# A routed feed-forward kernel: the high and low part of w2 side by side, streamed by one matmul of 512 columns

## The chip, the cores and the metric

The kernel runs on one core of one Trainium2 chip. A core has a matrix engine (TensorE: PE for its matmuls and PEld for its weight loads in the profile), VectorE (DVE), ScalarE (ACT), GpSimd (POOL), SyncE (SP), and 16 DMA engines. The metric is the device time of one execution in microseconds (us), as the median of several runs; lower is better. Durations of single instructions come from one profiled execution.

## The reference

A modulated linear layer makes a hidden vector for each of 8192 tokens; a router picks 2 of 8 experts for each token; each expert keeps at most 2560 tokens, runs a two-layer network on them, and the weighted result is added to the input.

```python
ys = cond * scale; d = rsqrt((ys * ys) @ (weight * weight) + EPS)
hidden = (x * ys[:, None, :]) @ weight * d[:, None, :]        # T = 8192 rows, D = 256
logits = hidden @ wr.T                                         # E = 8 experts
vals, idx = top_k(logits, 2);  gating = softmax over the two
dispatch = first cap (2560) tokens of each expert, in order of token
h = gelu(xg @ w1[e] + b1[e])                                   # F = 1024
y = h @ w2[e] + b2[e]                                          # D = 256
out = x + segment_sum(y * gate, dispatch)
```

## The kernel before

**Two stages.** Up to about 180 us of the profile the kernel makes the hidden rows, routes them, and writes a table of slots. After that it works through blocks of 256 slots (SLOTS, that is SUBS = 2 halves of 128 rows), expert by expert. Here there are 69 blocks, 8 or 9 of them for each of the 8 experts. The change lies in this second stage.

**Precision.** Weights and activations are split in two float32r parts: hi is the rounded value and lo the rest. A product takes three matmuls that add into the same PSUM columns: hi by hi, hi by lo and lo by hi (lines 522 to 524 for the first layer, 538 to 540 for the second).

**One block on TensorE** (`one_block`, line 547). Four transposes (line 512) bring in the rows of the next block. `first_product(f)`, for f = 0 to 7, makes 128 columns of h in a PSUM bank: 6 matmuls of 256 columns. `second_product(f)` adds the contribution of chunk f to y: for each of the two halves s the three matmuls 538 to 540, each with h as the loaded operand (128 rows) and 256 columns of w2 streamed, into `y_bank[s]` (banks 2 and 3, columns 0 to 255). A block has 48 + 48 such matmuls. The last matmul of f = 7 signals `y_done` for its half. The last two products of a block stand after the first two `first_product` of the next block. `second_product(0)` waits for `h_ready` of chunks 0 and 1 of its block (line 555); it is also what overwrites `y_bank`.

**The other engines.** ScalarE applies gelu to each bank of h twice (line 641, raw and hi). VectorE makes h_lo (line 902), then signals `h_ready`. At the end of a block VectorE's order, written by hand, is: h_lo of chunk 0 of the next block; for each half s wait for `y_free` and `y_done`, then y = bank + b2 (line 926); h_lo of chunk 1 of the next block (on which TensorE's `second_product(0)` waits); y times the gate (line 932), which signals `y_ready`.

**The way out** is GpSimd's (`one_block`, line 382, for each block): copy the slot numbers (line 370), issue the scatter-add of half 0 into the output (line 356), list the block three ahead (lines 331 and 332), issue its two gathers (line 323), issue the scatter-add of half 1 (line 356), wait until both adds have landed, and only then signal `y_free` (line 364). `y_sb` is single: VectorE's line 926 of a block waits for the landing of the block before.

**Weights.** In the first two blocks of an expert ScalarE (line 603) and VectorE (line 716) split the weights of the next expert from `w_raw`, 512 columns at a time, in 8 pieces. After the last piece SyncE loads the weights of the expert after that, 2 MB, into `w_raw`.

Of the kernel before, what the change touches and what calls it, by code (L numbers as in the profile page):

```python
# [24 lines left out]
P = 128  # L25
# [4 lines left out]
KC = D // P  # L30
# [20 lines left out]
PIECE = 512  # L51
PIECES = 2 * WCOLS // PIECE
PAD = SUBS * P
NO_SLOT = float(1 << 22)
# [3 lines left out]
def build(nc, x, cond, w, wr_t, w1, b1_t, w2, b2, ident, tri, expert_low, slot_base, token_ids,  # L58
# [12 lines left out]
    with ExitStack() as ctx:  # L71
# [69 lines left out]
        w_raw = sb("w_raw", [P, 2 * WCOLS])  # L141
        w_hi = [sb(f"w_hi{u}", [P, 2 * WCOLS], F32R) for u in range(2)]
        w_lo = [sb(f"w_lo{u}", [P, 2 * WCOLS], F32R) for u in range(2)]
        table_sb = sb("table", [P, COLS, 2], I32)
# [12 lines left out]
        h_hi = [sb(f"h_hi{i}", [P, SLOTS], F32R) for i in range(RING)]  # L157
        h_lo = [sb(f"h_lo{i}", [P, SLOTS], F32R) for i in range(RING)]
        y_sb = [sb(f"y{s}", [P, D]) for s in range(SUBS)]

# [53 lines left out]
        h_ready = sem("h_ready")  # L214
        y_done = sem("y_done")
        y_biased = sem("y_biased")
        y_ready = sem("y_ready")
# [9 lines left out]

        FILLING = GROUPS - 3

        def plan_of(eng, e):  # L230
# [198 lines left out]
        def _(pe):  # L429
# [86 lines left out]
            def first_product(u, f):  # L516

                h = h_bank[f % RING][:, 0:SLOTS]
                for k in range(KC):
                    cols = slice(k * F + f * P, k * F + (f + 1) * P)  # L520
                    rows = slice(k * SLOTS, (k + 1) * SLOTS)
                    pe.matmul(h, w_hi[u][:, cols], xt_hi[:, rows], start=(k == 0), stop=False)  # L522
                    pe.matmul(h, w_hi[u][:, cols], xt_lo[:, rows], start=False, stop=False)  # L523
                    mm = pe.matmul(h, w_lo[u][:, cols], xt_hi[:, rows], start=False, stop=(k == KC - 1))  # L524
                if f == FC - 1:
                    mm.then_inc(xt_used, 1)
                if f < RING:

                    mm.then_inc(h_open, 1)

            def second_product(u, f):

                cols = slice(WCOLS + f * D, WCOLS + (f + 1) * D)
                for s in range(SUBS):
                    hi = h_hi[f % RING][:, s * P:(s + 1) * P]
                    lo = h_lo[f % RING][:, s * P:(s + 1) * P]
                    y = y_bank[s][:, 0:D]
                    pe.matmul(y, hi, w_hi[u][:, cols], start=(f == 0), stop=False)  # L538
                    pe.matmul(y, hi, w_lo[u][:, cols], start=False, stop=False)  # L539
                    mm = pe.matmul(y, lo, w_hi[u][:, cols], start=False, stop=(f == FC - 1))  # L540
                    if f == FC - 1:
# [49 lines left out]
        def _(act):  # L591
# [7 lines left out]
            def split_piece(u, i, n_loaded):  # L599
                if i == 0:  # L600
                    act.wait_ge(w_loaded, n_loaded)
                cols = slice(i * PIECE, (i + 1) * PIECE)
                act.copy(w_hi[u][:, cols], w_raw[:, cols]).then_inc(w_hi_done, 1)

# [67 lines left out]
        def _(dve):  # L672
# [40 lines left out]
            def split_piece(u, i, count):  # L713
                cols = slice(i * PIECE, (i + 1) * PIECE)
                dve.wait_ge(w_hi_done, count)
                dve.tensor_tensor(w_lo[u][:, cols], w_raw[:, cols], w_hi[u][:, cols].bitcast(F32),
                                  ALU.subtract).then_inc(w_lo_done, 1)

# [193 lines left out]
            def one_block(u, e, b, tile, piece0):  # L912
# [9 lines left out]

                for s in range(SUBS):
                    dve.wait_ge(y_free, b * SUBS + (s + 1))
                    dve.wait_ge(y_done, b * SUBS + (s + 1))
                    dve.tensor_tensor(y_sb[s][:, :], y_bank[s][:, 0:D], b2_sb[:, bass.ds(e * D, D)],  # L926
                                      ALU.add).then_inc(y_biased, 1)
                split_chunk(b + 1, 1)
# [61 lines left out]
```

## Time and profile before

| what | us |
|---|---|
| median of 3 runs | 1146.6 |
| lowest and highest run | 1142.14, 1147.25 |
| span of the profiled execution, first to last instruction | 1087.6 |
| busy in that span: TensorE matmul, weight load | 986.6 (91%), 931.1 (86%) |
| busy: VectorE, ScalarE, GpSimd | 520.4 (48%), 552.6 (51%), 548.7 (50%) |

The median lies 59.0 us above the profiled span; that is time around the first and the last instruction that no row shows. A matmul's recorded duration (0.28 us here) includes its way through the array, and the next one starts before it ends: what a matmul costs in a stream is the distance from its start to the next one's. So a busy share of TensorE near 100% says that something was in the array, not that it was streaming at its peak. In brackets behind a row of the timeline stands the idle time of the engine before the row, and what ended it.

### The profile page before, as it was taken

What the parts mean: (1) busy time and instruction counts of PE and PEld (TensorE: products, weight loads), DVE (VectorE), ACT (ScalarE), POOL (GpSimd) and SP (SyncE); (2) the same over time, 40 slices, a digit from 0 to 9 for tenths busy, and PEclk for the clock granted to TensorE, in tenths of its full rate; (3) what the DMA queues carried; (4) which work ended last, traced back from release to release, by engine and by line L of the source; (5) the groups of instructions that cost most, each with busy time, mean ns of one, the idle gap of its engine ahead of it and who ended that gap; (6) DMA issues with size and microseconds to landing.
All of it is one profiled execution on the core that took longest, in us unless ns stands there. A gap on an engine that the chain in (4) does not pass through costs nothing.

```text
span 1087.6 us, 24164 instructions
## 1 busy us (share of the span) xinstructions
PE 986.6 (91%) x7652; PEld 931.1 (86%) x7653; DVE 520.4 (48%) x1555; ACT 552.6 (51%) x1312; POOL 548.7 (50%) x617
## 2 busy tenths in 40 slices
PE   6988883889989999899989998999899989999995
PEld 4656653789989999899989998999899989999995
DVE  5766664434454445344544444445444544345442
ACT  3111012646655657455646665556466655556553
POOL 0677777644444455344445454444445544445553
PEclk9888885989999999899989999999899999999998
DMA  8745415232242223322242224222422242222222
GB/s 281 242 146 174 136 60 166 75 72 43 39 117 39 43 48 80 69 44 43 39 116 39 44 47 111 43 43 39 116 39 43 43 115 44 43 39 39 40 47 29
DMA packets 70686, 83.62 MB, mean 77 GB/s; under 512 B 10944, under 2 KB 63680, under 8 KB 70528
## 3 DMA queue, kind: packets, MB, share of 16 engines
q0 software_dynamic: 30784, 36.86, 20.7%
q1 hardware_dynamic: 30064, 37.58, 10.5%
q10 hardware_dynamic: 9824, 9.03, 2.4%
q8 instruction: 5, 0.08, 0.0%
q14 instruction: 9, 0.07, 0.0%
HBM read 47.65 MB, written 35.69 MB: 77 GB/s over the span
## 4 chain that ended last, share of the span: by engine, by line
issue 31%; DMA 26%; POOL 22%; PE 7%; DVE 5%; POOLq 5%; DVEq 2%; SPq 1%; ACT 0%
DMA out_rows<-sb_y,sb_add_ids 24%; POOL sb_xg L323 8%; POOL table L316 6%; POOL sb_gather_ids L331 5%; DVE sb_y L932 2%; DVEq L932 2%; POOLq L331 2%; POOL sb_ids_ring L332 1%; PE bank L538 1%; POOL sb_add_ids L370 1%; PE bank L539 1%; PE bank L540 1%; DVE sb_y L926 1%; DMA table<-sb_pay,sb_slots 1%; DMA out_rows<-sb_x 1%
## 5 line engine op out<-in xcount | busy, mean ns | idle before, releaser
L641 ACT ACTIVATE sb_h_raw<-bank,sb_b_now 128x256 f32<-128x256 f32 x554 | 263.4, 475 | 370.0 <-PE bank L540 192.4
L902 DVE TENSOR_TENSOR sb_h_lo<-sb_h_raw,sb_h_hi 128x256 fp32r<-128x256 f32 x554 | 230.6, 424 | 301.5 <-ACT sb_h_hi L641 290.1
L538 PE MATMUL bank<-sb_w_hi,sb_h_hi 128*128 128x256 f32 x1104 | 318.5, 289 | 22.5 <-DVE sb_h_lo L902 22.2
L522 PE MATMUL bank<-sb_xt_hi,sb_w_hi 128*128 128x256 f32 x1108 | 322.7, 291 | 8.1 <-DVE sb_h_lo L902 5.4
L524 PE MATMUL bank<-sb_xt_hi,sb_w_lo 128*128 128x256 f32 x1108 | 315.3, 285 | 0.0
L523 PE MATMUL bank<-sb_xt_lo,sb_w_hi 128*128 128x256 f32 x1108 | 315.2, 284 | 0.0
L539 PE MATMUL bank<-sb_w_lo,sb_h_hi 128*128 128x256 f32 x1104 | 311.6, 282 | 0.0
L540 PE MATMUL bank<-sb_w_hi,sb_h_lo 128*128 128x256 f32 x1104 | 311.3, 282 | 0.0
L356 POOL DMA_INDIRECT out_rows<-sb_y,sb_add_ids x138 | 228.0, 1652 | 79.2 <-POOL sb_add_ids L370 53.0
L641 ACT ACTIVATE sb_h_hi<-bank,sb_b_now 128x256 fp32r<-128x256 f32 x554 | 259.7, 469 | 0.0
L538 PEld LDWEIGHTS bank<-sb_w_hi,sb_h_hi 128*128 128x128 f32 x1104 | 211.9, 192 | 32.3 <-DVE sb_h_lo L902 32.1
L522 PEld LDWEIGHTS bank<-sb_xt_hi,sb_w_hi 128*128 128x128 f32 x1108 | 213.3, 193 | 10.2 <-DVE sb_h_lo L902 7.0
L523 PEld LDWEIGHTS bank<-sb_xt_lo,sb_w_hi 128*128 128x128 f32 x1108 | 213.6, 193 | 0.0
L524 PEld LDWEIGHTS bank<-sb_xt_hi,sb_w_lo 128*128 128x128 f32 x1108 | 213.3, 192 | 0.0
L539 PEld LDWEIGHTS bank<-sb_w_lo,sb_h_hi 128*128 128x128 f32 x1104 | 211.4, 192 | 0.0
L540 PEld LDWEIGHTS bank<-sb_w_hi,sb_h_lo 128*128 128x128 f32 x1104 | 211.2, 191 | 0.0
L323 POOL DMA_INDIRECT sb_xg<-hidden,sb_gather_ids x134 | 135.3, 1010 | 83.2 <-POOL sb_ids_ring L332 55.7
L370 POOL COPY sb_add_ids<-sb_ids_ring 128x2 int32 x69 | 16.5, 239 | 299.6 <-DVE sb_y L932 299.6
L316 POOL DMA_INDIRECT table<-sb_pay,sb_slots x128 | 125.3, 979 | 68.1 <-issue 37.5
L926 DVE TENSOR_TENSOR sb_y<-bank,sb_b 128x256 f32<-128x256 f32 x138 | 52.2, 420 | 176.2 <-POOLq L364 165.6
L471 PE MATMUL bank<-sb_xs_t,sb_w 128*128 128x512 f32 x128 | 66.2, 666 | 0.0
L613 ACT COPY sb_hid<-bank 128x512 f32<-128x512 f32 x32 | 17.2, 588 | 91.2 <-PE bank L491 91.2
(110 smaller groups left out, 778.4 us busy)
## 6 DMA issues: line engine op xcount, KB each, us to landing
sb_w_raw<-in_w SPq DMA_DIRECT2D x18, 1024.0 KB
out_rows<-sb_x SPq DMA_DIRECT2D x16, 512.0 KB
hidden<-sb_hid ACTq DMA_DIRECT2D x16, 512.0 KB
sb_x<-in_x SPq DMA_DIRECT2D x15, 512.0 KB
out_rows<-sb_y,sb_add_ids POOLq DMA_INDIRECT x138
sb_xg<-hidden,sb_gather_ids POOLq DMA_INDIRECT x134
table<-sb_pay,sb_slots POOLq DMA_INDIRECT x128
sb_b<-in_b SPq DMA_DIRECT2D x1, 1024.0 KB, 8.9
```

Source lines behind the costliest of these rows:

```text
L316: pool.indirect_dma_start(table, bass.IndirectOffsetOnAxis(slots[u][:, c, j:j + 1], axis=0), pay[u][:, c, j, :], None, bounds_check=TABLE ...
L323: pool.indirect_dma_start(into[:, s, :], None, hidden, bass.IndirectOffsetOnAxis(block_ids[:, s:s + 1], axis=0),).then_inc(landed, 16)
L331: pool.tensor_copy(gather_ids[:, :], ids)
L356: pool.indirect_dma_start(out, bass.IndirectOffsetOnAxis(add_ids[:, s:s + 1], axis=0), y_sb[s][:, :], None, compute_op=ALU.add,).then_inc( ...
L522: pe.matmul(h, w_hi[u][:, cols], xt_hi[:, rows], start=(k == 0), stop=False)
L523: pe.matmul(h, w_hi[u][:, cols], xt_lo[:, rows], start=False, stop=False)
L524: mm = pe.matmul(h, w_lo[u][:, cols], xt_hi[:, rows], start=False, stop=(k == KC - 1))
L538: pe.matmul(y, hi, w_hi[u][:, cols], start=(f == 0), stop=False)
L539: pe.matmul(y, hi, w_lo[u][:, cols], start=False, stop=False)
L540: mm = pe.matmul(y, lo, w_hi[u][:, cols], start=False, stop=(f == FC - 1))
L641: ins = act.activation(h[f % RING][:, :], h_bank[f % RING][:, 0:SLOTS], ACT.Gelu_apprx_tanh, bias=b1_now[u][:, f:f + 1])
L902: dve.tensor_tensor(h_lo[f % RING][:, :], h_raw[f % RING][:, :], h_hi[f % RING][:, :].bitcast(F32), ALU.subtract).then_inc(h_ready, 1)
```

## The change

w1 keeps its two buffers of hi and lo parts, now under names of their own. For w2 the hi and the lo part of each chunk f lie side by side in one buffer `w2_both[P, FC, 2, D]`, so that 512 columns follow one another. `second_product` streams those 512 columns through the loaded h_hi into the whole bank: columns 0 to 255 get hi by hi, columns 256 to 511 get hi by lo. A second matmul loads h_lo and adds lo by hi into the upper half. The output y is then the sum of the two halves of the bank and b2. VectorE first adds b2 to the upper half into a new tile `y_low` (waiting for `y_done` alone), for both halves s, and then adds `y_low` to the lower half into `y_sb` (waiting for `y_free`). Blocks stay at 256 slots; loops, gelu, the first product and GpSimd's program are as they were.

```diff
-        w_hi = [sb(f"w_hi{u}", [P, 2 * WCOLS], F32R) for u in range(2)]
-        w_lo = [sb(f"w_lo{u}", [P, 2 * WCOLS], F32R) for u in range(2)]
+        w1_hi = [sb(f"w1_hi{u}", [P, WCOLS], F32R) for u in range(2)]
+        w1_lo = [sb(f"w1_lo{u}", [P, WCOLS], F32R) for u in range(2)]
+        w2_both = [sb(f"w2_both{u}", [P, FC, 2, D], F32R) for u in range(2)]
...
+        def piece_of(u, i):
+
+            if i < W1_PIECES:
+                cols = slice(i * PIECE, (i + 1) * PIECE)
+                return w1_hi[u][:, cols], w1_lo[u][:, cols], w_raw[:, cols]
+            chunks = PIECE // D
+            f = (i - W1_PIECES) * chunks
+            raw = w_raw[:, i * PIECE:(i + 1) * PIECE].rearrange("p (c d) -> p c d", d=D)
+            return w2_both[u][:, f:f + chunks, 0, :], w2_both[u][:, f:f + chunks, 1, :], raw
...
             def second_product(u, f):
 
-                cols = slice(WCOLS + f * D, WCOLS + (f + 1) * D)
+                both = w2_both[u][:, f, :, :].rearrange("p v d -> p (v d)")
                 for s in range(SUBS):
                     hi = h_hi[f % RING][:, s * P:(s + 1) * P]
                     lo = h_lo[f % RING][:, s * P:(s + 1) * P]
-                    y = y_bank[s][:, 0:D]
-                    pe.matmul(y, hi, w_hi[u][:, cols], start=(f == 0), stop=False)
-                    pe.matmul(y, hi, w_lo[u][:, cols], start=False, stop=False)
-                    mm = pe.matmul(y, lo, w_hi[u][:, cols], start=False, stop=(f == FC - 1))
+                    pe.matmul(y_bank[s][:, :], hi, both, start=(f == 0), stop=False)
+                    mm = pe.matmul(y_bank[s][:, D:2 * D], lo, w2_both[u][:, f, 0, :], start=False, stop=(f == FC - 1))
...
                 for s in range(SUBS):
+                    dve.wait_ge(y_done, b * SUBS + (s + 1))
+                    dve.tensor_tensor(y_low[s][:, :], y_bank[s][:, D:2 * D], b2_sb[:, bass.ds(e * D, D)],
+                                      ALU.add).then_inc(y_begun, 1)
+                for s in range(SUBS):
+                    dve.wait_ge(y_begun, b * SUBS + (s + 1))
                     dve.wait_ge(y_free, b * SUBS + (s + 1))
-                    dve.wait_ge(y_done, b * SUBS + (s + 1))
-                    dve.tensor_tensor(y_sb[s][:, :], y_bank[s][:, 0:D], b2_sb[:, bass.ds(e * D, D)],
-                                      ALU.add).then_inc(y_biased, 1)
+                    dve.tensor_tensor(y_sb[s][:, :], y_bank[s][:, 0:D], y_low[s][:, :], ALU.add).then_inc(y_biased, 1)
```

On TensorE, `second_product(6)` at the end of a block, the kernel before:

```order
L538 MATMUL bank2<-sb_w_hi1,sb_h_hi2 128x256 [waits h_ready]
L539 MATMUL bank2<-sb_w_lo1,sb_h_hi2 128x256
L540 MATMUL bank2<-sb_w_hi1,sb_h_lo2 128x256
L538 MATMUL bank3<-sb_w_hi1,sb_h_hi2 128x256
L539 MATMUL bank3<-sb_w_lo1,sb_h_hi2 128x256
L540 MATMUL bank3<-sb_w_hi1,sb_h_lo2 128x256
```

and the changed one, with the first two matmuls of the next product behind it (its lines are numbered anew):

```order
L551 MATMUL bank2<-sb_w2_both1,sb_h_hi2 128x512 [waits h_ready]
L552 MATMUL bank2<-sb_w2_both1,sb_h_lo2 128x256
L551 MATMUL bank3<-sb_w2_both1,sb_h_hi2 128x512
L552 MATMUL bank3<-sb_w2_both1,sb_h_lo2 128x256
L536 MATMUL bank5<-sb_xt_hi,sb_w1_hi1 128x256
L537 MATMUL bank5<-sb_xt_lo,sb_w1_hi1 128x256
```

Six matmuls with six weight loads became four with four; the streamed columns are the same 1536.

On VectorE, at the end of a block, the kernel before:

```order
L902 TENSOR_TENSOR sb_h_lo0<-sb_h_raw0,sb_h_hi0 128x256 [waits gelu_done]
L924 ISA
L926 ISA [waits y_done,y_free]
L926 TENSOR_TENSOR sb_y0<-bank2,sb_b2 128x256
L924 REGISTER_ALU
L926 TENSOR_TENSOR sb_y1<-bank3,sb_b2 128x256 [waits y_done,y_free]
L901 REGISTER_ALU
L902 TENSOR_TENSOR sb_h_lo1<-sb_h_raw1,sb_h_hi1 128x256 [waits gelu_done]
```

and the changed one:

```order
L913 TENSOR_TENSOR sb_h_lo0<-sb_h_raw0,sb_h_hi0 128x256 [waits gelu_done]
L935 ISA
L936 ISA [waits y_done]
L936 TENSOR_TENSOR sb_y_low0<-bank2,sb_b2 128x256
L935 REGISTER_ALU
L936 TENSOR_TENSOR sb_y_low1<-bank3,sb_b2 128x256 [waits y_done]
L941 TENSOR_TENSOR sb_y0<-bank2,sb_y_low0 128x256 [waits y_free,y_begun]
L941 TENSOR_TENSOR sb_y1<-bank3,sb_y_low1 128x256 [waits y_free,y_begun]
L912 REGISTER_ALU
L913 TENSOR_TENSOR sb_h_lo1<-sb_h_raw1,sb_h_hi1 128x256 [waits gelu_done]
```

Two additions of the same size were put ahead of the two that were there; the wait for `y_free` now stands between them, and h_lo of chunk 1 stands behind all four.

## Rows read from the trace of the kernel before

**Rows 1.** Page, busy time of each engine with its share of the span, and instructions.

```profile
PE 986.6 (91%) x7652; PEld 931.1 (86%) x7653; DVE 520.4 (48%) x1555; ACT 552.6 (51%) x1312; POOL 548.7 (50%) x617
```

**Rows 2.** Waits of VectorE, 205 to 1088 us: total, times, longest.

```profile
DVE sb_y L926 <- POOLq L364: 165.6, 62, 6.4
...
DVE sb_y L926 <- POOLq L410: 7.4, 1, 7.4
DVE sb_y L926 <- PE bank L540: 3.2, 6, 0.5
```

**Rows 3.** Timeline of VectorE, 836 to 849 us: start, us, instruction, idle before.

```profile
836.35 0.76 DVE L926 TENSOR_TENSOR sb_y<-bank,sb_b 128x256 f32<-128x256 f32 x2 [2.49 <-POOLq L364]
...
837.39 0.82 DVE L932 TENSOR_SCALAR sb_y<-sb_y,sb_table 128x256 f32<-128x256 f32 x2
...
840.77 0.42 DVE L902 TENSOR_TENSOR sb_h_lo<-sb_h_raw,sb_h_hi 128x256 fp32r<-128x256 f32 x1 [0.99 <-ACT sb_h_hi L641]
...
848.59 0.42 DVE L926 TENSOR_TENSOR sb_y<-bank,sb_b 128x256 f32<-128x256 f32 x1 [2.46 <-POOLq L364]
```

**Rows 4.** Timeline of GpSimd, the same stretch.

```profile
838.05 0.20 POOL L370 COPY sb_add_ids<-sb_ids_ring 128x2 int32 x1 [4.00 <-DVE sb_y L932]
839.09 1.60 POOL L356 DMA_INDIRECT out_rows<-sb_y,sb_add_ids  x1 [0.84 <-POOL sb_add_ids L370]
...
840.23 0.99 POOL L332 COPY sb_ids_ring<-sb_table  x1
842.11 1.01 POOL L323 DMA_INDIRECT sb_xg<-hidden,sb_gather_ids  x1 [0.88 <-POOL sb_ids_ring L332]
...
844.70 1.61 POOL L356 DMA_INDIRECT out_rows<-sb_y,sb_add_ids  x1 [0.30 <-issue]
```

**Rows 5.** Timeline of TensorE, 834 to 838 us.

```profile
834.35 0.28 PE L540 MATMUL bank<-sb_w_hi,sb_h_lo 128*128 128x256 f32 x1
...
835.77 0.28 PE L524 MATMUL bank<-sb_xt_hi,sb_w_lo 128*128 128x256 f32 x1
...
837.49 0.38 PE L538 MATMUL bank<-sb_w_hi,sb_h_hi 128*128 128x256 f32 x1 [0.30 <-DVE sb_h_lo L902]
```

**Rows 6.** Line 471 (float32, 512 columns): TensorE, 90 to 94 us.

```profile
90.56 3.60 PE L471 MATMUL bank<-sb_xs_t,sb_w 128*128 128x512 f32 x8
```

**Rows 7.** Timeline of VectorE's line 926, from one expert's first blocks to the next one's.

```profile
324.47 0.76 DVE L926 TENSOR_TENSOR sb_y<-bank,sb_b 128x256 f32<-128x256 f32 x2 [6.09 <-POOLq L364]
...
337.05 0.78 DVE L926 TENSOR_TENSOR sb_y<-bank,sb_b 128x256 f32<-128x256 f32 x2 [0.53 <-PE bank L540]
...
349.43 0.76 DVE L926 TENSOR_TENSOR sb_y<-bank,sb_b 128x256 f32<-128x256 f32 x2 [1.20 <-POOLq L364]
...
361.54 0.76 DVE L926 TENSOR_TENSOR sb_y<-bank,sb_b 128x256 f32<-128x256 f32 x2 [1.60 <-POOLq L364]
...
373.65 0.75 DVE L926 TENSOR_TENSOR sb_y<-bank,sb_b 128x256 f32<-128x256 f32 x2 [2.00 <-POOLq L364]
...
386.02 0.76 DVE L926 TENSOR_TENSOR sb_y<-bank,sb_b 128x256 f32<-128x256 f32 x2 [2.58 <-POOLq L364]
```

**Rows 8.** Windows: engines' busy time (instructions), TensorE's granted clock, DMA share, GB/s.

```profile
320.00:324.00 4.00, 1.86 (x15) 1.59 (x14) 0.00 (x0) 1.48 (x4) 0.00 (x0) 0.97 0.89 278
324.00:328.00 4.00, 2.63 (x13) 2.39 (x12) 2.28 (x7) 0.70 (x2) 1.03 (x2) 0.50 0.01 2
```

**Rows 9.** Timeline of TensorE, 328 to 330 us, at the lower granted clock.

```profile
328.34 0.41 PE L538 MATMUL bank<-sb_w_hi,sb_h_hi 128*128 128x256 f32 x1
328.56 0.41 PE L539 MATMUL bank<-sb_w_lo,sb_h_hi 128*128 128x256 f32 x1
```

**Rows 10.** Timeline of GpSimd, 361 to 374 us: the copy of line 332.

```profile
365.45 0.75 POOL L332 COPY sb_ids_ring<-sb_table  x1
```

**Rows 11.** Timeline of VectorE, the last block.

```profile
1074.90 0.77 DVE L926 TENSOR_TENSOR sb_y<-bank,sb_b 128x256 f32<-128x256 f32 x2 [0.53 <-PE bank L540]
```

More of the change, by code:

```diff
@@ L52 @@
 PIECES = 2 * WCOLS // PIECE
+W1_PIECES = WCOLS // PIECE
 PAD = SUBS * P
@@ L158, in build @@
         h_lo = [sb(f"h_lo{i}", [P, SLOTS], F32R) for i in range(RING)]
+        y_low = [sb(f"y_low{s}", [P, D]) for s in range(SUBS)]
         y_sb = [sb(f"y{s}", [P, D]) for s in range(SUBS)]
@@ L215, in build @@
         y_done = sem("y_done")
+        y_begun = sem("y_begun")
         y_biased = sem("y_biased")
@@ L521, in first_product @@
                     rows = slice(k * SLOTS, (k + 1) * SLOTS)
-                    pe.matmul(h, w_hi[u][:, cols], xt_hi[:, rows], start=(k == 0), stop=False)
-                    pe.matmul(h, w_hi[u][:, cols], xt_lo[:, rows], start=False, stop=False)
-                    mm = pe.matmul(h, w_lo[u][:, cols], xt_hi[:, rows], start=False, stop=(k == KC - 1))
+                    pe.matmul(h, w1_hi[u][:, cols], xt_hi[:, rows], start=(k == 0), stop=False)
+                    pe.matmul(h, w1_hi[u][:, cols], xt_lo[:, rows], start=False, stop=False)
+                    mm = pe.matmul(h, w1_lo[u][:, cols], xt_hi[:, rows], start=False, stop=(k == KC - 1))
                 if f == FC - 1:
@@ L601, in split_piece @@
                     act.wait_ge(w_loaded, n_loaded)
-                cols = slice(i * PIECE, (i + 1) * PIECE)
-                act.copy(w_hi[u][:, cols], w_raw[:, cols]).then_inc(w_hi_done, 1)
+                hi, _, raw = piece_of(u, i)
+                act.copy(hi, raw).then_inc(w_hi_done, 1)
             for i in range(PIECES):
@@ L713, in split_piece @@
             def split_piece(u, i, count):
-                cols = slice(i * PIECE, (i + 1) * PIECE)
+                hi, lo, raw = piece_of(u, i)
                 dve.wait_ge(w_hi_done, count)
-                dve.tensor_tensor(w_lo[u][:, cols], w_raw[:, cols], w_hi[u][:, cols].bitcast(F32),
-                                  ALU.subtract).then_inc(w_lo_done, 1)
+                dve.tensor_tensor(lo, raw, hi.bitcast(F32), ALU.subtract).then_inc(w_lo_done, 1)
             dve.wait_ge(const_in, 16 * CONSTS)
```

## The prediction

> **What bounds the kernel now.** The page comes first, and it misleads. TensorE is busy 91% of the span and its weight loads 86%, every other engine about half [rows 1]. Read alone, that says TensorE is the bound and every nanosecond taken off its stream is time won. So the second view is the waits, and there VectorE's line 926, the step that takes a finished block out of the bank. It needs two things: `y_done` (TensorE has finished the block) and `y_free` (the scatter-adds of the block before have landed). In 62 of 69 blocks the later of the two was GpSimd's signal, 165.6 us of waiting in all; one more is the first block, released once by line 410. Only in 6 blocks was TensorE the later one, and all 6 together waited 3.2 us, at most 0.5 us each [rows 2]. 62 + 1 + 6 is all of them. The reader should see that TensorE, busy as it looks, is early nearly always.
>
> The third view is one turn of what is late instead. From line 926 at 836.35 us to the next at 848.59 us is 12.24 us [rows 3]. In between: the gate at 837.39 [rows 3], GpSimd's copy at 838.05, the add of half 0 issued at 839.09, the first gather at 842.11, the add of half 1 at 844.70 [rows 4], and 3.9 us later both adds have landed and the next 926 starts. Nothing in this circle is a matmul. TensorE's own work for a block is 96 matmuls at a distance of 0.118 us (834.35 to 835.77 us is twelve starts [rows 5]), 11.3 us, and with the four transposes 11.7 us. That is 0.5 us less than the turn; TensorE takes the difference as a wait for h_lo of chunk 1, which stands behind 926 (the row at 837.49 [rows 5]). In that turn the last matmul of `second_product(7)` started at 834.35 and ends its 0.28 us at 834.63; 926 started 1.7 us later.
>
> TensorE leads only in short episodes. After an expert's first two blocks SyncE loads 2 MB of weights; in 320 to 324 us the DMA share is 0.89 at 278 GB/s, and after it TensorE's granted clock is 0.50, the 1.2 GHz level [rows 8]. The adds land late, 926 waits 6.09 us, TensorE stands, and the next block starts at the low clock, so that its 926, at 337.05, is released by TensorE after 0.53 us of idling. From then on TensorE, at 11.7 us a block, runs ahead of the circle again: the idle time before 926 is 1.20, 1.60, 2.00, 2.58 us [rows 7].
>
> **The change part by part.** *Removed on TensorE:* 2 weight loads and 2 matmuls in each `second_product`, while the streamed columns stay the same. A group of three costs 3 x 0.118 = 0.353 us now. At the lower clock the distance is 0.22 us, as read to two places (328.34 to 328.56 [rows 9]), about 256 cycles of 1.2 GHz (0.213 us): one column a cycle. At the upper clock 256 columns need 0.107 us, so 0.011 us of each 0.118 is not streaming. The trace has no float32r matmul of 512 columns. The lower bound is pure streaming, 0.213 us; the upper is twice the narrow one, 0.236 us; a middle, 0.219 us, takes 0.353 to 0.337 us and saves 0.016 us a group (bounds 0 and 0.023). A farther bound is line 471, whose float32 matmuls of 512 columns leave two records each in the trace, 8 records in 3.60 us, 0.45 us a record [rows 6]; with it a group would cost 0.57 us. I exclude most of that because those need more than one pass, and the float32r ones of rows 9 need one. So TensorE's work falls by 16 x 0.016 = 0.26 us a block, 69 x 0.26 = 18 us in all. Where the circle leads, this turns into idle time before 926 and is worth nothing. The cover is 1.7 us of lead in the steady turn.
>
> *Added on VectorE:* two additions a block, ahead of the wait for `y_free`. Two of this shape take 0.76 us together, the second starting 0.34 us after the first [rows 3]. Behind them stand the final additions, h_lo of chunk 1 (TensorE waits for it), the gate, and behind that GpSimd. Where the idle time before 926 is 1.2 us or more, they fit into it: 0.53 us until half 0 is done, 0.36 us (three matmuls) until half 1 is, 0.34 us to the next start is 1.23 us. That holds for 63 of 69 blocks, and costs nothing there beyond a few hundredths. In the 6 TensorE-led blocks the final addition starts 0.36 + 0.34 = 0.70 us later than it did, less the 0.02 us that the old pair lost waiting for half 1 (0.78 instead of 0.76 us [rows 7]), less what TensorE gained since it was last released: about 0.15 us in the five after a weight load, where part of the block runs at the low clock (a group is 768 cycles either way), and 0.26 us in the last block of all, which is led by TensorE too [rows 11]. Net 5 x (0.68 - 0.15) + (0.68 - 0.26) = 3.1 us **later**.
>
> *Moved:* GpSimd's copy at line 332 takes 0.99 us in the steady turn [rows 4], where VectorE's line 902 at 840.77 us [rows 3] falls into it, and 0.75 us in a turn where TensorE is less far ahead [rows 10]. The turns show it: 361.54 to 373.65 is 12.11 us, 373.65 to 386.02 is 12.37 us; the step comes when the idle time before 926 passes about 2 us [rows 7]. After the change TensorE reaches that lead sooner (0.26 us more a block, and 0.5 us more because the led block ended later), so one short turn fewer after each of the five episodes: 5 x 0.25 = 1.2 us later. The new additions read one operand from PSUM; the rule for this is in the Trainium skill, SBUF — State Buffer, section Who interferes with whom: a VectorE instruction with two SBUF inputs contends with a GpSimd one that reads SBUF, one with a single SBUF input does not. Rows 4 and 10 agree on line 902, which has two; no row shows the new pair beside a copy. By the rule it costs GpSimd nothing.
>
> *The split of w2* writes the same 512 columns in two pieces of 256 and stays as long. SyncE's and GpSimd's programs are untouched. Buffers are as large as before.
>
> Sum: + 3.1 + 1.2 = + 4.3 us on the profiled span of 1087.6 us, 1091.9 us. The median of the runs stands 59.0 us above that span, and the change touches none of that: 1146.6 + 4.3 = **1150.9 us**.
>
> **The rivals.** *TensorE is the bound after all.* Then all 18 us come out at the end: 1146.6 - 18 = 1129 us. For it speaks rows 1; against it rows 2, where a TensorE that were infinitely fast could remove 3.2 us of waiting before 926. The Trainium skill (Perfetto Trace Analysis, section Identifying the Most-Contended Engine) says to optimize first the engine with the highest occupancy and to judge TensorE by its weight-load share; by that rule this rival would be the forecast, and the waits of this trace disagree. Chance 0.09.
>
> *The low clock lasts longer (the other side).* In the window at 324 us TensorE is busy 2.63 of 4 us and at 0.50 [rows 8]. A shorter stream makes the idle time around each weight load longer by some 0.3 us. If one more stretch of about 3.5 us ran at 1.2 GHz after each of the 7 episodes, the block would lose half of it, 1.7 us. It decides there because TensorE leads, with 0.5 us and less to spare; in a steady turn the lead of 1.7 us would cover it. Price 7 x 1.7 = 12 us: 1163 us. Chance 0.08.
>
> *VectorE is late in every block.* If in the steady turn the new pair ended after `y_free`, the circle would grow by up to 0.7 us, 63 x 0.7 = 44 us: 1195 us. It needs `y_done` to come 1 us later than it does. Chance 0.02.
>
> *The wide matmul doesn't stream at one column a cycle.* At 0.45 us a group costs 0.57 us, TensorE's block 11.7 + 16 x 0.21 = 15.1 us, above 12.24: about 2.9 us x 69 = 200 us, 1347 us. The point from which it decides is a group of 0.353 + 0.53 / 16 = 0.386 us. Chance 0.02.
>
> **How the numbers follow.** A measurement of this kernel can tell about 0.5% from no change, 5.7 us: 1140.9 to 1152.3 us. The forecast case has 0.79. Its own bounds: with no saving in the wide matmul, + 1.0 us; with two short turns lost instead of one, + 1.2; with none of the new delay because the episodes fall differently in a run, - 4.3; the two runs farthest apart differ by 5.1 us, and a change in where line 902 meets the copies by 0.1 us a turn is 7 us either way. It therefore gives 1142 to 1159 us, and splits into 0.54 same, 0.23 slower, 0.02 faster. Adding the rivals: faster 0.11, same 0.54, slower 0.35. The range 1142 to 1160 leaves out the first rival, most of the second, and the two far ones.
>
> **What would show each step.** In the changed profile: TensorE's distance from line 551 to 552 near 0.219 us and from 552 on near 0.118; TensorE's and the weight loads' busy shares lower; the idle time before the final additions still ended by line 364 in some 62 blocks; turns of 12.1 to 12.4 us, as before; the first additions started before `y_free` in those; the final additions 0.5 us later in the blocks after a weight load. I am wrong if turns are shorter than 12.1 us in number, which would mean that TensorE's work reaches the circle by a way I have not seen, or if they are longer than 12.4 us outside the episodes.

## The result and the profile after

| | kernel before | changed kernel |
|---|---|---|
| median of 16 runs each, us | 1143.6 | 1148.8 |
| profiled execution, us (its span) | not known (1087.6) | 1150.9 (1149.1) |

The ratio of the two, runs on the same chips against each other, is **1.0053, 95% interval 1.0031 to 1.0076**: about 6 us slower (the two medians are 5.2 us apart). One of the 16 runs of the changed kernel took 1898.6 us and is not in the ratio. The forecast was 4.3 us slower, 1150.9 us. It started from the three runs of before shown then, whose median was 1146.6 us; with 13 more it is 1143.6.

The page of the changed kernel, to be read against [rows 1]:

```profile
PE 1002.7 (87%) x6548; PEld 892.0 (78%) x6549; DVE 574.0 (50%) x1693; ACT 553.8 (48%) x1312; POOL 549.7 (48%) x617
```

1104 matmuls and weight loads fewer, and VectorE has 138 instructions and 53.6 us more. The busy shares tell nothing of the time: TensorE's work fell and the kernel got slower. VectorE's waits, the counterpart of [rows 2] (us in total, times, longest), 260 to 1149 us:

```profile
DVE sb_y L941 <- POOLq L378: 103.9, 61, 5.5
...
DVE sb_y_low L936 <- PE bank L552: 29.6, 66, 0.6
```

The final addition (line 941) is still released by GpSimd's signal (line 378) in 61 blocks. What was one wait of 165.6 us is now a short wait for TensorE ahead of the new additions (line 936) and a shorter one for GpSimd behind them. One turn, VectorE, 324 to 328 us (start, us, instruction, idle before), beside [rows 3]:

```profile
324.41 0.78 DVE L936 TENSOR_TENSOR sb_y_low<-bank,sb_b 128x256 f32<-128x256 f32 x2 [0.45 <-PE bank L552]
...
326.49 0.76 DVE L941 TENSOR_TENSOR sb_y<-bank,sb_y_low 128x256 f32<-128x256 f32 x2 [1.30 <-POOLq L378]
327.16 0.41 DVE L913 TENSOR_TENSOR sb_h_lo<-sb_h_raw,sb_h_hi 128x256 fp32r<-128x256 f32 x1
327.54 0.82 DVE L946 TENSOR_SCALAR sb_y<-sb_y,sb_table 128x256 f32<-128x256 f32 x2
```

The new pair has ended 1.30 us before the final additions start, so it is hidden there, as forecast. TensorE, 650 to 652 us, beside [rows 5]:

```profile
650.78 0.50 PE L551 MATMUL bank<-sb_w_both,sb_h_hi 128*128 128x512 f32 x1 [0.43 <-DVE sb_h_lo L913]
...
651.23 0.39 PE L551 MATMUL bank<-sb_w_both,sb_h_hi 128*128 128x512 f32 x1
651.46 0.28 PE L552 MATMUL bank<-sb_w_both,sb_h_lo 128*128 128x256 f32 x1
651.58 0.28 PE L536 MATMUL bank<-sb_xt_hi,sb_w_hi 128*128 128x256 f32 x1
```

The second wide matmul stands 0.23 us before its successor (median 0.231), a narrow one 0.12 (0.118). A group is 0.349 us. The three narrow ones of the second product were 0.351 us by their medians (0.118, 0.116, 0.117); the forecast took 3 x 0.118.

**Where the 6 us are.** Three sums over the trace make up the time from the first block's final addition to the last block's: the way round from there to `y_free`; the delay from `y_free` to the next final addition where GpSimd is the later; and the same delay where TensorE is.

| us | before | changed | difference | forecast |
|---|---|---|---|---|
| first final addition to last | 869.3 | 876.4 | +7.1 | +4.3 |
| final addition to `y_free`, 68 turns | 862.1 | 863.6 | +1.4 | +1.2 |
| `y_free` to final addition, TensorE later | 4.4 (6 blocks) | 6.7 (7 blocks) | +2.2 | +3.1 |
| the same, GpSimd later | 2.7 (62 blocks) | 6.1 (61 blocks) | **+3.4** | 0 |

Half of the difference is in a row that the forecast doesn't have. It is also the only row that doesn't hang on one execution: against a second profile of the kernel before (below) the four differences are +3.6, -4.4, +4.6 and +3.3. Median of that delay: 0.031 us before, 0.101 us after. The chain of waits shows what fills it (start, us, what). First the kernel before, 836 to 836.5 us:

```profile
832.44 3.84 DMA out_rows<-sb_y,sb_add_ids
836.27 0.02 issue
836.30 0.03 POOLq L364
836.32 0.02 issue
836.35 0.05 DVE sb_y L926
```

then the changed one, 326 to 326.6 us:

```profile
322.56 3.79 DMA out_rows<-sb_y,sb_add_ids
326.35 0.02 issue
326.37 0.03 POOLq L378
326.39 0.03 issue
326.42 0.02 DVEq L940
326.44 0.04 issue
326.49 0.06 DVE sb_y L941
```

Before, the addition starts right behind GpSimd's signal. After, a semaphore instruction of VectorE's own sequencer (DVEq L940) stands between the two. Both additions have two semaphores to wait for. In the kernel before, the wait for `y_free` is written first and `y_done` second; in the changed one `y_begun` is first and `y_free` second. The wait that is written first is carried by the addition, the other becomes an instruction ahead of it. So the suspicion is that neither the wide matmul nor the four additions cost these 3.4 us, but the order of two lines.

### The profile page after: what moved, and what is told of

It reads as the page before. It is cut to its first block, busy times and chain, and to the rows that moved or that the text cites. A ratio compares the mean times of both kernels' runs of the same rounds, so it can differ in the third digit from the quotient of the medians.

```text
span 1149.1 us, 22094 instructions
## 1 busy us (share of the span) xinstructions
PE 1002.7 (87%) x6548; PEld 892.0 (78%) x6549; DVE 574.0 (50%) x1693; ACT 553.8 (48%) x1312; POOL 549.7 (48%) x617
## 4 chain that ended last, share of the span: by engine, by line
issue 26%; DMA 23%; POOL 16%; PE 11%; DVE 9%; another core or an unknown queue 8%; POOLq 4%; DVEq 3%; SPq 0%; ACT 0%
DMA out_rows<-sb_y,sb_add_ids 22%; POOL sb_xg L337 7%; POOL sb_gather_ids L345 5%; PE bank L551 3%; DVE sb_y L946 2%; DVEq L946 2%; POOLq L345 2%; PE bank L552 1%; POOL sb_ids_ring L346 1%; POOL table L330 1%; DVE sb_y L941 1%; POOL sb_add_ids L384 1%; PE bank L485 1%; PE bank L536 1%
## 5 line engine op out<-in xcount | busy, mean ns | idle before, releaser
L551 PE MATMUL bank<-sb_w_both,sb_h_hi 128*128 128x512 f32 x1104 | 415.5, 403 | 29.7 <-DVE sb_h_lo L913 29.6
L552 PE MATMUL bank<-sb_w_both,sb_h_lo 128*128 128x256 f32 x1104 | 312.8, 283 | 0.0
L551 PEld LDWEIGHTS bank<-sb_w_both,sb_h_hi 128*128 128x128 f32 x1104 | 210.7, 191 | 70.5 <-DVE sb_h_lo L913 40.4
L552 PEld LDWEIGHTS bank<-sb_w_both,sb_h_lo 128*128 128x128 f32 x1104 | 211.5, 192 | 0.0
L941 DVE TENSOR_TENSOR sb_y<-bank,sb_y_low 128x256 f32<-128x256 f32 x138 | 52.0, 419 | 103.9 <-POOLq L378 103.9
L485 PE MATMUL bank<-sb_xs_t,sb_w 128*128 128x512 f32 x128 | 71.5, 710 | 0.5 <-DVE sb_xs_t L692 0.5
L936 DVE TENSOR_TENSOR sb_y_low<-bank,sb_b 128x256 f32<-128x256 f32 x138 | 53.4, 423 | 30.7 <-PE bank L552 30.2
L346 POOL COPY sb_ids_ring<-sb_table (+1 forms) x67 | 63.1, 941 | 0.0
```

The costliest lines, as they stand in the source:

```text
L485: mm = pe.matmul(bank[2 + o][:, :], w_sb[:, k, o * P:(o + 1) * P], xs_t[:, k, :], start=(k == 0), stop=(k == KC - 1))
L551: pe.matmul(y_bank[s][:, :], hi, both, start=(f == 0), stop=False)
L552: mm = pe.matmul(y_bank[s][:, D:2 * D], lo, w2_both[u][:, f, 0, :], start=False, stop=(f == FC - 1))
```

## Experiments: the parts of the change one by one

The first four ran on one chip against the same 35 runs of the kernel before (median 1141.4 us). To compare the traces without the first stage, which differs from execution to execution (below), each also has its time from the **second** block's final addition to the last: 853.2 us in the profile of before, 855.3 in another one of the same kernel (below), 860.3 after.

**The two waits exchanged in the changed kernel.**

```diff
-                    dve.wait_ge(y_begun, b * SUBS + (s + 1))
                     dve.wait_ge(y_free, b * SUBS + (s + 1))
+                    dve.wait_ge(y_begun, b * SUBS + (s + 1))
```

> The changed kernel with the two waits before the final addition written in the other order: y_free first, then y_begun. In the trace of the changed kernel the wait for y_free is an instruction of its own and the addition starts 0.10 us after GpSimd's signal; before, it sat on the addition and that took 0.03 us. Theory: the circle y_free, addition, gate, adds, y_free sets the time, and the 0.07 us in each of 62 turns are 4.3 us of the change's 6 us; swapped, the start is 0.03 us after the signal again and the ratio to before 1.0015 to 1.002. Rival (the 0.07 us come from the two new additions or from what TensorE does then, not from the order of the waits): 1.005 as before, start still 0.10 us after the signal.

Measured: 1143.9 us, ratio 1.0039 [1.0013, 1.0066]. In the trace the addition starts 0.032 us behind the signal, as expected, and the stretch takes 854.5 us. The ratio missed its 1.0015 to 1.002 and lies nearer to the rival's 1.005; the interval holds both.

**The waits exchanged in the kernel before.**

```diff
-                    dve.wait_ge(y_free, b * SUBS + (s + 1))
                     dve.wait_ge(y_done, b * SUBS + (s + 1))
+                    dve.wait_ge(y_free, b * SUBS + (s + 1))
```

> The kernel before with the two waits of line 926 written in the other order, y_done first, then y_free, and nothing else. Theory: the wait for y_free becomes an instruction of its own, the addition starts 0.10 instead of 0.03 us after GpSimd's signal, 62 turns make 4.3 us: ratio 1.0035 to 1.004. Rival (the order of waits is worth nothing): 1.000.

Measured: 1144.8 us, 1.0016 [0.9986, 1.0047]; delay 0.102 us, stretch 858.5 us. The chain at 623 us:

```profile
619.52 3.81 DMA out_rows<-sb_y,sb_add_ids
623.33 0.02 issue
623.35 0.03 POOLq L364
623.38 0.03 issue
623.40 0.02 DVEq L925
623.43 0.04 issue
623.47 0.07 DVE sb_y L926
```

It is the picture of the changed kernel, line for line, without anything else of the change: L925 is now ahead of the addition. The mechanism is shown. Its size in the times is not: each exchange moved the ratio by some 0.15%, less than half of the 0.4% that 62 turns of 0.07 us would be, and the intervals hold both that and nothing.

**VectorE's part alone:** three narrow matmuls again, and the four additions.

```diff
-                    pe.matmul(y_bank[s][:, :], hi, both, start=(f == 0), stop=False)
+                    pe.matmul(y_bank[s][:, 0:D], hi, w2_both[u][:, f, 0, :], start=(f == 0), stop=False)
+                    pe.matmul(y_bank[s][:, D:2 * D], hi, w2_both[u][:, f, 1, :], start=False, stop=False)
                     mm = pe.matmul(y_bank[s][:, D:2 * D], lo, w2_both[u][:, f, 0, :], start=False, stop=(f == FC - 1))
```

> The changed kernel with three matmuls of 256 columns again (hi by hi into the lower half, the other two into the upper half); VectorE's four additions stay. This is VectorE's part of the change alone. Theory: what the wide matmul saves TensorE (0.353 to 0.348 us a group, 0.1 us a block) is idle time, so this kernel is as slow as the changed one, ratio 1.005 to 1.006. Rival (TensorE's saving reaches the end): 69 x 0.1 = 7 us slower than the changed kernel, 1.011.

Measured: 1148.0 us, 1.0051 [1.0017, 1.0084], as expected; delay 0.102 us, stretch 859.0 us. That is the whole change's 1.0053, without the wide matmul.

**TensorE's part alone:** the wide matmul, and only the lower half of the bank is added to b2. The upper half is left out of y.

```diff
-                    dve.wait_ge(y_done, b * SUBS + (s + 1))
-                    dve.tensor_tensor(y_low[s][:, :], y_bank[s][:, D:2 * D], b2_sb[:, bass.ds(e * D, D)],
-                                      ALU.add).then_inc(y_begun, 1)
...
-                    dve.wait_ge(y_begun, b * SUBS + (s + 1))
                     dve.wait_ge(y_free, b * SUBS + (s + 1))
-                    dve.tensor_tensor(y_sb[s][:, :], y_bank[s][:, 0:D], y_low[s][:, :], ALU.add).then_inc(y_biased, 1)
+                    dve.wait_ge(y_done, b * SUBS + (s + 1))
+                    dve.tensor_tensor(y_sb[s][:, :], y_bank[s][:, 0:D], b2_sb[:, bass.ds(e * D, D)],
+                                      ALU.add).then_inc(y_biased, 1)
```

> The wide matmul alone: TensorE as in the changed kernel, VectorE as before, with one addition a half (y = lower half + b2) and the old waits. It leaves out the upper half of the bank, so that y lacks the hi by lo and lo by hi terms. Theory: nothing of TensorE's saving arrives but some hundredths in the blocks that TensorE leads: 0.999 to 1.000. Rival (TensorE is the bound): 7 us less, 0.994. Rival (the wide matmul hurts by itself, by idle time and a low clock for longer): above 1.002.

Measured: 1145.0 us, 1.0018 [0.9984, 1.0051]; delay 0.032 us, stretch 852.2 us. Its waits of VectorE, 250 to 1140 us, read like [rows 2]:

```profile
DVE sb_y L937 <- POOLq L378: 171.8, 65, 6.3
...
DVE sb_y L937 <- PE bank L552: 2.2, 4, 0.6
```

The stretch is 1.0 and 3.1 us shorter than in the two profiles of the kernel before, which are themselves 2.1 us apart; in the times the wide matmul alone is worth nothing that they can tell. The ratio missed the expected 0.999 to 1.000, and its interval doesn't exclude that the wide matmul hurts. VectorE still waits for GpSimd in 65 blocks: a shorter stream of TensorE leaves that wait where it was (171.8 us, against 165.6 and 182.0 us in the two profiles of before).

**Three of them again.** Intervals of 0.3% either way do not tell 0.2% from 0.4%, so three kernels ran again, the first two on one chip (23 runs of before, 1142.6 us), the third on another (17 runs, 1141.7 us).

> The kernel before with the two waits of line 926 in the other order, once more, since 1.0016 with an interval of 0.9986 to 1.0047 told nothing. Its trace showed the addition 0.10 us behind GpSimd's signal in place of 0.03. Theory: 62 to 66 turns x 0.07 us are 4.5 us, ratio 1.004. Rival (taken up elsewhere): 1.000.

> The wide matmul with the one addition and the waits of the kernel before, once more (1.0018, interval 0.9984 to 1.0051). It leaves out the upper half of the bank, so that y lacks the hi by lo and lo by hi terms. Theory: 0.999 to 1.000. Rival (the wide matmul hurts by itself): above 1.002.

> The changed kernel with y_free waited for first, once more (1.0039, interval 1.0013 to 1.0066; its trace had the addition 0.03 us behind the signal, and 854.5 us from the second block's addition to the last one's in place of 860.3). Theory: of the change's 6 us the waits' order is 4.3, what is left is 2 to 3 us, ratio 1.002 to 1.003. Rival (the order is worth nothing in the time): 1.005.

The second and third came out as expected, though the third's interval still holds the rival's 1.005; the first lies between its theory's 1.004 and its rival's 1.000 and excludes neither. With the first round beside them:

| kernel | ratio, first | ratio, again | delay behind the signal, us | stretch, us | median turn, us |
|---|---|---|---|---|---|
| before | 1 | 1 | 0.031, 0.031 | 853.2, 855.3 | 12.34, 12.34 |
| wide matmul alone | 1.0018 [0.9984, 1.0051] | 0.9996 [0.9971, 1.002] | 0.032, 0.032 | 852.2, 850.8 | 12.32, 12.33 |
| before, waits exchanged | 1.0016 [0.9986, 1.0047] | 1.0025 [0.9994, 1.0056] | 0.102, 0.102 | 858.5, 857.0 | 12.43, 12.39 |
| changed, waits exchanged | 1.0039 [1.0013, 1.0066] | 1.0022 [0.999, 1.0053] | 0.032, 0.031 | 854.5, 854.5 | 12.34, 12.32 |
| VectorE's part alone | 1.0051 [1.0017, 1.0084] | | 0.102 | 859.0 | 12.42 |
| changed | 1.0053 [1.0031, 1.0076] | | 0.101 | 860.3 | 12.42 |

A turn is the time from one block's final addition to the next block's. The traces fall into two groups by the order of the waits: with `y_free` first the stretch is 850.8 to 855.3 us and the median turn 12.32 to 12.34 us, with it second 857.0 to 860.3 us and 12.39 to 12.43 us. So the 0.07 us do arrive in the steady turn, whatever else of the change is there. The ratios point the same way in both pairs, by 0.1 to 0.3% instead of the 0.4% that 62 x 0.07 = 4.3 us would be. What is shown: the wide matmul brings nothing that can be told; VectorE's part alone is as slow as the whole change; and the order of the waits lengthens the turn. How much of the 0.5% in the times is the order's is not resolved: the middle values give it some two fifths, and the intervals hold everything from nothing to most of it.

## Experiments: is the circle the bound, and what is outside the span

**The kernel before once more.** The forecast had put 59.0 us of the median outside the profiled span.

> The kernel before once more, for a second profile. The first one spans 1087.6 us where its runs take 1146.6, and its blocks begin at 187 us; the changed kernel's spans 1149.1, and its blocks begin at 249 us. Theory: the short first stage belongs to that one execution, and this profile spans about 1142 us with its blocks from about 245 us; from the second block's addition to the last one's it takes 853 us as in the first profile (860 in the changed kernel). Rival: the kernel before really has a first stage of 180 us, and 59 us lie outside of the instructions.

Measured: 1094.8 us, span 1093.0 us. Both readings missed: the first stage is short again, as the rival had it, but only 1.8 us lie outside the span, here and in the changed kernel (1150.9 and 1149.1). But nine runs of before on this chip have a median of 1093.6 us, on the other three chips it is 1141.4, 1142.6 and 1141.7 us. So it is not an accident of one execution either; as far as these four chips show, it goes with the chip. The traces show where it is: in the first gather of a block's rows (its engine, times, first and last start), before, then changed:

```profile
L323 POOL DMA_INDIRECT sb_xg_first<-hidden,sb_ids_ring x2: 967/985/1003, 173.9 to 175.4; - x2
```

```profile
L337 POOL DMA_INDIRECT sb_xg_first<-hidden,sb_ids_ring x2: 974/990/1007, 213.7 to 215.2; - x2
```

40 us are lost ahead of the first block's gather. The first final addition then stands at 205.6 and 260.1 us, 54.5 us apart. The kernel before shows the same on such a chip (its exchanged forms: 259.4 and 258.2 us). The loss is spread over the stage: ScalarE copies the hidden rows out of the bank 16 times, 9.5 us apart on average in the first profile of before and 12.9 us apart in the changed kernel's. In a window of the changed kernel's trace in which the kernel before was well into its blocks (windows: engines' busy time with instructions, granted clock, DMA share, GB/s), before and then changed:

```profile
220.00:240.00 20.00, 18.24 (x136) 18.04 (x135) 8.17 (x21) 8.56 (x21) 8.18 (x11) 0.83 0.23 35
```

```profile
220.00:240.00 20.00, 0.00 (x0) 0.00 (x0) 7.30 (x31) 0.00 (x0) 15.20 (x16) 0.50 0.07 16
```

The change doesn't touch that stage's work, but the stage adds scatter to the ratios: in the ten profiles where it is long, the first final addition stands at 256.5 to 261.9 us. Why it takes longer on some chips is open.

**The circle broken.** If the circle through line 926 is the bound, it should help to take work out of it. The addition writes a tile of its own, `y_pre`, and waits for `y_done` alone; only the gate, which writes `y_sb`, waits for `y_free`.

```diff
-                    dve.wait_ge(y_free, b * SUBS + (s + 1))
                     dve.wait_ge(y_done, b * SUBS + (s + 1))
-                    dve.tensor_tensor(y_sb[s][:, :], y_bank[s][:, 0:D], b2_sb[:, bass.ds(e * D, D)],
+                    dve.tensor_tensor(y_pre[s][:, :], y_bank[s][:, 0:D], b2_sb[:, bass.ds(e * D, D)],
...
+                    dve.wait_ge(y_free, b * SUBS + (s + 1))
-                    dve.tensor_scalar(y_sb[s][:, :], y_sb[s][:, :],
+                    dve.tensor_scalar(y_sb[s][:, :], y_pre[s][:, :],
```

> The kernel before, with line 926 writing to a tile of its own and waiting for y_done alone; the gate step (line 932) reads that and waits for y_free. So two additions and h_lo of chunk 1 leave the circle through GpSimd. Theory (the circle is the bound): it falls from 12.24 to about 11.2 us, below TensorE's 11.7 us a block, TensorE becomes the bound in most blocks, some 50 blocks x 0.5 us and 1 us in each of 14 slow turns make about 35 us: ratio 0.967 to 0.975. Rival (TensorE is the bound already): 1.000.

Measured: 1052.0 us against 1093.6, **0.9624 [0.961, 0.9637]**. That is a larger gain than the expected 0.967 to 0.975. Nothing was taken off TensorE, the engine that is busy 91%, and 41.5 us went. The Trainium skill (Perfetto Trace Analysis, section Identifying the Most-Contended Engine) would have the busiest engine optimized first. If that is read as taking work off it, the runs disagree: its work cut brought nothing, the wait moved brought 3.8%. VectorE in a steady turn:

```profile
499.60 0.77 DVE L926 TENSOR_TENSOR sb_y_pre<-bank,sb_b 128x256 f32<-128x256 f32 x2 [0.46 <-PE bank L541]
...
502.66 0.35 DVE L933 TENSOR_SCALAR sb_y<-sb_y_pre,sb_table 128x256 f32<-128x256 f32 x1 [1.95 <-issue]
...
511.56 0.78 DVE L926 TENSOR_TENSOR sb_y_pre<-bank,sb_b 128x256 f32<-128x256 f32 x2 [0.46 <-PE bank L541]
```

The addition is now TensorE's to release (0.46 us), the turn is 11.96 us, and the gate waits. Its wait ends in "issue" and not in GpSimd's signal, because behind the signal stand the instructions that work out where in the table the gate is read, about 0.5 us; the gate starts 0.61 us behind the signal (median). The circle is still a little longer than the 11.72 us that TensorE needs for a block when nothing holds it (from the last matmul of half 0 to the same one a block later).

**The same on the changed kernel.** Here the wide matmul should at last be worth its saving.

```diff
                 for s in range(SUBS):
                     dve.wait_ge(y_begun, b * SUBS + (s + 1))
-                    dve.wait_ge(y_free, b * SUBS + (s + 1))
-                    dve.tensor_tensor(y_sb[s][:, :], y_bank[s][:, 0:D], y_low[s][:, :], ALU.add).then_inc(y_biased, 1)
+                    dve.tensor_tensor(y_pre[s][:, :], y_bank[s][:, 0:D], y_low[s][:, :], ALU.add).then_inc(y_biased, 1)
...
+                    dve.wait_ge(y_free, b * SUBS + (s + 1))
-                    dve.tensor_scalar(y_sb[s][:, :], y_sb[s][:, :],
+                    dve.tensor_scalar(y_sb[s][:, :], y_pre[s][:, :],
```

> The same edit on the changed kernel: y_low and the sum go to tiles of their own and wait for TensorE alone, the gate step waits for y_free. Theory: TensorE is the bound now, so the wide matmul's 0.1 us a block (11.72 to 11.62 us) arrives: 4 to 6 us faster than the same edit on the kernel before, 0.963 to 0.970. Rival (the wide matmul is worth nothing even then, or VectorE's two more additions delay h_lo of chunk 1): equal to it or slower.

Measured: 1057.6 us, 0.9673 [0.966, 0.9687]: 5.6 us slower than the same edit on the kernel before, the expectation missed, sign and all. The median turn is 12.00 us against 11.97, so the circle still bound both. TensorE's waits for h_lo of chunk 1, which stands behind four additions instead of two: first the kernel before with the edit, then the changed one.

```profile
PE bank L523 <- DVE sb_h_lo L903: 14.2, 21, 1.4
```

```profile
PE bank L537 <- DVE sb_h_lo L914: 16.3, 23, 1.7
```

That is 2.1 us, about what the spans of the two profiles are apart (1050.1 and 1051.9). The profiled execution of the changed one was its fastest (1053.7); where the other 4 us of its median come from, no trace shows.

**The gate's table value fetched ahead.** To take the 0.5 us out of the circle too, the gate's two columns are copied to a small tile before the wait for `y_free`. On the kernel before:

```diff
+                dve.tensor_copy(gate_now[:, :], table_sb.bitcast(F32)[:, bass.ds(tile, SUBS), 1]).then_inc(gate_read, 1)
+                dve.wait_ge(gate_read, b + 1)
...
+                    dve.wait_ge(y_free, b * SUBS + (s + 1))
-                    dve.tensor_scalar(y_sb[s][:, :], y_sb[s][:, :],
-                                      table_sb.bitcast(F32)[:, bass.ds(tile + s, 1), 1],
+                    dve.tensor_scalar(y_sb[s][:, :], y_pre[s][:, :],
+                                      gate_now[:, s:s + 1],
```

> The kernel before with the gate step waiting for y_free, and with the block's gate column copied to a fixed tile ahead of that wait, so that no address is worked out between y_free and the gate step. In the version without the copy the turns were 11.7 to 12.0 us, and the gate step started about 0.5 us after y_free. Theory (the circle is the bound wherever a turn is above 11.72 us): some 35 turns lose 0.25 us and the slow turns 0.4 us each, 10 to 15 us less than without the copy, ratio 0.949 to 0.955. Rival (those turns are set by something else): 0.962 as without the copy.

Measured: 1087.2 us against 1142.6 on this chip, **0.9505 [0.9471, 0.9539]**, 55 us less, inside the expected 0.949 to 0.955 and the best ratio of all kernels here. One turn:

```profile
604.77 0.76 DVE L928 TENSOR_TENSOR sb_y_pre<-bank,sb_b 128x256 f32<-128x256 f32 x2 [0.27 <-PE bank L543]
...
606.15 0.17 DVE L932 COPY sb_gate_now<-sb_table 128x2 f32 x1
607.12 0.61 DVE L937 TENSOR_SCALAR sb_y<-sb_y_pre,sb_gate_now 128x256 f32<-128x256 f32 x2 [0.81 <-POOLq L367]
...
616.28 0.78 DVE L928 TENSOR_TENSOR sb_y_pre<-bank,sb_b 128x256 f32<-128x256 f32 x2 [0.26 <-PE bank L543]
```

The gate now starts 0.09 us behind the signal (median), and its two halves take 0.61 us where they took 0.82 [rows 3]; the 0.30 us of address work between addition and gate (DVEq L932 in the chain of before) is gone from the circle. This turn of VectorE is 11.51 us; the median is 11.72, and TensorE's own distance from one block's last matmul of half 0 to the next one's is 11.71 to 11.72 us in three of four turns. Now TensorE is the bound.

**And on the changed kernel,** the same edit.

> The changed kernel with the same two edits: the gate step waits for y_free, its column is copied ahead. Theory: TensorE is the bound in most turns, and the wide matmul's 0.05 us a block (11.72 to 11.66 us in the turns that nothing else holds) arrives: 2 to 4 us faster than the same edits on the kernel before. Rival (even where TensorE is the bound the two more additions on VectorE cost more than that): equal or slower, as it was without the copy, 1057.6 against 1052.0 us.

Measured: 1092.0 us, 0.9567 [0.9528, 0.9606], 4.7 us more than with narrow matmuls where 2 to 4 less were expected. The final additions' first and last start, narrow and wide:

```profile
L928 DVE TENSOR_TENSOR sb_y_pre<-bank,sb_b x138: 411/424/426, 256.8 to 1071.7; 128x256 f32<-128x256 f32 x138
```

```profile
L943 DVE TENSOR_TENSOR sb_y_pre<-bank,sb_y_low x138: 411/414/417, 261.6 to 1076.2; 128x256 f32<-128x256 f32 x138
```

In the two profiles the blocks take the same: 814.9 and 814.6 us. All that parts them, 4.8 us, is in the stage ahead. The steady turn did get shorter (median 11.68 against 11.72 us, TensorE's distance alone 0.06 us a block, some 4 us in all), but TensorE's waits took nearly all of it: for the gathers' rows behind the weight loads, and for h_lo behind the four additions. Narrow first (257 to 1072 us), then wide (262 to 1076 us):

```profile
PE bank L515 <- DMA sb_xg<-hidden,sb_gather_ids: 10.7, 7, 2.5
PE bank L525 <- DVE sb_h_lo L905: 1.4, 4, 0.6
```

```profile
PE bank L529 <- DMA sb_xg<-hidden,sb_gather_ids: 11.6, 7, 2.3
PE bank L539 <- DVE sb_h_lo L916: 4.1, 8, 1.0
```

(11.6 + 4.1) - (10.7 + 1.4) = 3.6 us. So even with TensorE as the bound the wide matmul is worth about nothing in the blocks. Whether the 4.7 us of the medians are more than the first stage's scatter between executions is not settled.

## Why the prediction was right, and where not

*The circle is the bound, TensorE is early in 62 + 1 of 69 blocks.* Right, and shown by more than the waits: cutting TensorE's stream changed nothing that can be told (1.0018 and 0.9996), cutting the circle gave 3.8 and 5.0%.

*The wide matmul saves 0.016 us a group.* Mis-sized: its distance is 0.231 us where the middle of the bounds was taken, 0.219. It is near the upper bound, twice the narrow one's, 0.236. The two narrow matmuls that it replaces took 0.234 us, so the saving is 0.002 to 0.004 us a group; TensorE's block, where nothing holds it, is 11.66 instead of 11.72 us, 4 us in all instead of 18. Nothing hung on it here, since the circle led.

*The new additions hide in the idle time.* Right: 1.30 us were left in a steady turn after 0.78 us of additions. In the blocks that TensorE leads they are exposed as described, the final pair 0.69 us behind the first:

```profile
392.03 0.78 DVE L936 TENSOR_TENSOR sb_y_low<-bank,sb_b 128x256 f32<-128x256 f32 x2 [0.45 <-PE bank L552]
392.72 0.75 DVE L941 TENSOR_TENSOR sb_y<-bank,sb_y_low 128x256 f32<-128x256 f32 x2
```

The forecast was 3.1 us for the six of them; in the changed kernel's trace they are seven, and the difference is 2.2 us (4.6 against the second profile of before, in which TensorE leads only two blocks).

*One short turn fewer in five episodes, 1.2 us.* The sum that holds it grew by 1.4 us. That is no proof of the mechanism: in the second profile of before the same sum is 867.9 us, 5.8 more than in the first, so it scatters by more than the term. And the short turns are not fewer once the order of the waits is taken out: between 12.00 and 12.25 us lie 17 and 18 turns in the two profiles of before, 15 and 19 in the two of the changed kernel with the waits exchanged. That the sum fitted was luck.

*"It costs nothing there beyond a few hundredths."* **This is the step that failed.** The few hundredths were put at nothing in the sum; they are 0.07 us in each of some 62 blocks, +3.4 us in the trace and 4.3 by 62 x 0.07, the largest single term. The prediction's own sign speaks of it: it called itself wrong if turns grew longer than 12.4 us outside the episodes, and the median turn went from 12.34 to 12.42 us. The order listing ahead of the prediction shows both waits on one addition; the code shows `y_free` written first before and second after. What came of it was not asked. The chain of before would have raised the question: 0.02 us and no other instruction stand between the signal and the addition. How much of it is in the times, the experiments leave open.

*The median stands 59.0 us above the span as time around the first and last instruction.* Wrong. It was a profile from a chip with a short first stage beside runs from chips with a long one. The predicted time was not hurt, since the difference was added to the median, but a change in the first stage would have been priced on the wrong trace.

*The rivals.* TensorE as bound (1129 us), a longer low clock, VectorE late everywhere and a wide matmul that does not stream are all out. TensorE's mean granted clock from 300 to 1000 us (the last number but two), before and then changed:

```profile
300.00:1000.00 700.00, 665.07 (x5457) 654.89 (x5456) 319.94 (x763) 412.81 (x985) 335.05 (x384) 0.98 0.30 59
```

```profile
300.00:1000.00 700.00, 660.55 (x4563) 610.94 (x4561) 355.93 (x863) 410.14 (x978) 330.84 (x378) 0.98 0.30 59
```

It is 0.98 in both.

*The sum.* +4.3 was forecast and about +6 measured (0.53%). That they are near is partly luck: the terms that were there came out at 3.6 instead of 4.3, and against the second profile of before at 0.2; only the missing one, +3.4, is the same against both.

## What to carry to other kernels

Find the engine that is late at the wait where the stages meet, and price a change by what it does on that circle; a busy share of 91% was no sign that the engine was the bound. Where an instruction waits for two semaphores, write first the one that comes last, and look in the chain for what stands between its signal and the instruction. When a circle bounds, first look for work in it that doesn't need the contended buffer: letting the gate instead of the addition wait for `y_free`, and fetching its operand ahead, brought nine times what all the parts of this change moved.

## What the runs showed of the hardware

- Two waits on one VectorE instruction are not equal. It starts 0.03 us after the signal of the semaphore that is written first, and 0.10 us after that of the one written second.
- A register offset costs time between a signal and the instruction: 0.61 us from `y_free` to a gate that reads the table at a computed place, and 0.09 us once the value is fetched ahead.
- A float32r matmul of 512 columns with its weight load takes 0.231 us of the stream, the two of 256 that it replaces took 0.234: the longer matmul gained about 1%.
- The same kernel took 1093.6 us on one chip and 1141 to 1143 us on three others, all of it ahead of the first block's final addition. Ratios hold only within a chip.
